# A fused attention and quantised feed-forward kernel: new instruction orders on all engines, the inverse roots apart, fillers on TensorE, the last sets woven

## The chip, the cores and the metric

One core of a Trainium2 chip. The metric is the device time of one execution in microseconds. The kernel before takes 356.12 us (median of 3 runs, 355.98 to 356.35).

## What is computed

Rows are 8192 tokens (32 x 256) of 256 values. The attention mask leaves each query only the keys whose index is congruent to its own modulo the number of queries. Here both counts are 256, so exactly one key is left, the softmax is 1, and attention is a product of the context with Wv and Wout. Wq and Wk have no effect.

```
x = x + tanh(g_xattn) * ((ctx @ Wv) @ Wout + bout)
h = layernorm(layernorm(x)) * ln1_g + ln1_b
h = bitlinear(h, w1, b1)             # 256 -> 1024
h = gelu(h)
h = layernorm(h) * ln2_g + ln2_b
x = x + tanh(g_ffn) * bitlinear(h, w2, b2)   # 1024 -> 256
bitlinear: rows rounded to 8-bit steps of max|row|/127, weights to -1, 0, 1 times mean|w|
```

## The kernel before

The tokens form S = 16 sets; a set is 128 partitions x T = 4 tiles of rows. Wv and Wout are multiplied once into `wvo` (256 x 256), both weight matrices are rounded and transposed on the chip. After that the kernel is a software pipeline of bodies i = -3 to 17. Body i works on several sets at once: the attention of set i+3 (TensorE, L1028), the residual and first statistics of set i+2 (VectorE, L734, L745), the first norm of set i+1, the hidden product and Gelu of set i (L1099, L572), the second norm and its quantising of set i-1 (rows L776, maxima L780), and the second product and the output of sets i-2 and i-3 (L1112, L823).

There is no scheduler. Each engine runs an instruction list written by hand, and semaphores tie the lists together; a wait blocks everything behind it on its engine. So the order in each `body(i)` is what decides who is late. The parts that the change touches:

- GpSimd (L372 to L483). `gain` (L395) multiplies one 128x1024 tile by ln2_g, four times a body; `gain_first` (L386) is one pass as large; `norm_first` (L403, L404) prepares the first variance. `variance` (L413, L414) waits for the fourth squared sum and then makes mean and variance of the second norm. `root` (L378) takes the power -0.5 of both variances, 128x8, in one instruction. `deviations` (L421) and five `split` steps (L437, L442) write means, deviations and scales as three bf16 parts each into `parts`.
- TensorE. `turn_rows` (L1059) transposes `parts` into PSUM, ScalarE copies them (`take_rows`, L563), and then `correction` (L1070, two matmuls into `slot_c`) makes the rank-few terms of a row: the mean and shift of the second norm. `slot_c` holds one row's terms, so a correction waits until VectorE has taken the one before. `hidden` (L1096, L1099) is the first product of a tile, `second_product` and `second_bias` (L1112, L1118) the second, `turn_context` (L948) and `attention` (L1028, L1032) the attention of a half set.
- VectorE. `row` adds the correction to the tile, `row_max` takes its maximum, `final` (L823) writes an output tile. `scales` (L794 to L811) makes quantising scales from maxima and roots in six small operations; its last one, L811, releases ScalarE's `quantise_first` (L544) and GpSimd's `split` of the next body.
- ScalarE. Four pairs of `gelu` (L572) and `square` (L580) a body, the quantising copies (L544, L553), and the copies out of PSUM.
- SyncE (SP) issues the loads, stores and the transposing transfers that turn a quantised tile for the second product (`turn_second`, L243) and the first (`turn_first`, L235), in one queue order. A transfer whose wait isn't met holds up all that stand behind it.

Attention ends at set 15, so TensorE has none from body 13 on. At the end the last set goes through `row`, `scales`, `quantise`, transpose, product and output with little beside it. Its statistics come from one root over four tiles.

## Time and profile before

| what | value |
|---|---|
| median of 3 runs | 356.12 us |
| profiled execution | 356.32 us, its span 354.5 us (1.8 us lie around the span) |
| mean granted TensorE clock | 0.957 of full |
| TensorE busy | 296.9 us, 84% |
| VectorE busy | 294.9 us, 83% |
| ScalarE busy | 277.2 us, 78% |
| GpSimd busy | 265.2 us, 75% |
| DMA | 51.57 MB, mean 145 GB/s |

All engines are busy for three quarters of the span or more, and none is full. In such a kernel the busy share tells little. What is read instead is one body of the pipeline: how long it is, and which chain through the engines closes upon itself in just that time. "Idle before" in a timeline row is the time for which the engine stood still ahead of it, with the instruction that ended the wait. The granted clock of TensorE is 1.00 at 2.4 GHz and 0.50 at 1.2 GHz.

### The profile page before, as it was taken

The page shows a single profiled execution, that of the slowest core. Times are in us where ns is not written, and L with a number is a line of the kernel's source. Part 1 is how long each engine was busy: PE and PEld are TensorE (multiplying, and loading weights), DVE is VectorE, ACT ScalarE, POOL GpSimd, SP SyncE. Part 2 cuts the span into 40 slices and gives each one's busy share as a digit, 9 for nine tenths or more (in the row PEclk, how much of TensorE's full clock was granted, in tenths as well). Part 3 has the DMA queues.
Part 4 walks back from the last instruction along what each step waited for, and adds up shares of the span by engine and source line. Part 5 has one row for each costly group of instructions (what it writes and reads, how often), then busy time and mean ns, then how long its engine had stood idle before and what let it go on. Part 6 is the DMA issues. An engine that isn't in the chain of part 4 may idle for free. (4 is left out here: it accounts for less than half of the span.)

```text
span 354.5 us, 5862 instructions
## 1 busy us (share of the span) xinstructions
PE 296.9 (84%) x1680; PEld 191.7 (54%) x1704; DVE 294.9 (83%) x521; ACT 277.2 (78%) x444; POOL 265.2 (75%) x298
## 2 busy tenths in 40 slices
PE   5998887889898979898989899989998849394566
PEld 4867463537475646465656565655655424242344
DVE  0268898989999999999999999989999948666582
ACT  2155696898989899998989898989898977779340
POOL 4045789997989888989898989898898986738410
PEclk9999999989999999999999999999999978978598
DMA  7956513364858685768666767595555445361457
GB/s 220 324 188 252 151 61 89 118 150 119 189 131 182 111 204 138 170 157 145 182 154 159 160 164 152 165 150 150 112 97 106 104 95 114 74 133 38 82 115 213
DMA packets 98634, 51.57 MB, mean 145 GB/s; under 512 B 87097, under 2 KB 89588, under 8 KB 98602
## 3 DMA queue, kind: packets, MB, share of 16 engines
q1 hardware_dynamic: 97706, 51.15, 59.5%
q8 instruction: 14, 0.23, 0.3%
q10 hardware_dynamic: 896, 0.04, 0.2%
q14 instruction: 18, 0.15, 0.1%
HBM read 21.79 MB, written 8.41 MB: 85 GB/s over the span
## 5 line engine op out<-in xcount | busy, mean ns | idle before, releaser
L395 POOL TENSOR_TENSOR y<-u,g_bc 128x1024 f32<-128x1024 f32 x64 | 151.0, 2368 | 15.3 <-ACT u L572 14.3
L776 DVE TENSOR_TENSOR y<-y,slot_c 128x1024 f32<-128x1024 f32 x64 | 77.7, 1214 | 23.3 <-PE slot_c L1070 23.3
L780 DVE TENSOR_REDUCE amax<-y 128x1 f32<-128x1024 f32 x64 | 78.0, 1218 | 1.8
L553 ACT ACTIVATE q<-y,scale 128x1024 f16<-128x1024 f32 x64 | 70.0, 1144 | 8.2 <-DVE scale L811 8.2
L580 ACT ACTIVATE junk<-u,usum 128x1024 bf16<-128x1024 f32 x64 | 73.7, 1151 | 2.0
L1112 PE MATMUL bank_f<-w2T,q2T 128*128 128x256 f16 x448 | 60.7, 281 | 7.4 <-DVE res L823 5.5
L1112 PEld LDWEIGHTS bank_f<-w2T,q2T 128*128 128x128 f16 x448 | 44.6, 101 | 23.5 <-DVE res L823 6.1
L1028 PE MATMUL slot_a<-wvo,ctxT 128*128 128x256 f32 x208 | 53.4, 386 | 1.0 <-ACT ctxT L515 1.0
L1070 PE MATMUL slot_c<-ln_rows,rows 128*128 128x512 bf16 x119 | 38.1, 397 | 16.6 <-ACT rows L563 7.2
L572 ACT ACTIVATE u<-slot_a,d 128x1024 f32<-128x1024 f32 x32 | 35.5, 1109 | 10.8 <-PE slot_a L1099 9.3
L1028 PEld LDWEIGHTS slot_a<-wvo,ctxT 128*128 128x128 f32 x208 | 36.3, 190 | 11.1 <-ACT ctxT L515 3.6
L1099 PE MATMUL slot_a<-w1T,q1T 128*128 128x512 f16 x128 | 40.5, 400 | 0.5 <-issue 0.2
L544 ACT ACTIVATE q<-h,scale 128x256 f16<-128x256 f32 x64 | 27.4, 500 | 13.8 <-DVE scale L811 13.8
L1099 PE MATMUL slot_b<-w1T,q1T 128*128 128x512 f16 x128 | 38.1, 380 | 0.0
L386 POOL TENSOR_TENSOR h<-x,g_bc 128x1024 f32<-128x1024 f32 x15 | 35.5, 2368 | 0.0
L572 ACT ACTIVATE u<-slot_b,d 128x1024 f32<-128x1024 f32 x32 | 35.1, 1097 | 0.0
L378 POOL TENSOR_TENSOR rstd<-var,half_neg 128x8 f32<-128x8 f32 x18 | 30.2, 1675 | 2.4
L1070 PEld LDWEIGHTS slot_c<-ln_rows,rows 128*128 128x128 bf16 x128 | 10.3, 99 | 33.9 <-issue 17.3
L823 DVE SCALAR_TENSOR_TENSOR res<-bank_f,d,x 128x256 f32<-128x256 f32 x56 | 24.4, 478 | 3.4 <-PE bank_f L1118 3.4
L745 DVE BATCH_NORM_STATS2 bn<-x 128x6 f32<-128x256 f32 x64 | 24.1, 418 | 1.0
L1096 PE MATMUL slot_b<-b_rows,rows 128*128 128x512 bf16 x64 | 24.5, 383 | 0.0
L515 ACT COPY ctxT<-bank_q 128x512 f32<-128x512 f32 x32 | 18.3, 572 | 6.2 <-PE bank_q L948 6.2
(136 smaller groups left out, 430.9 us busy)
## 6 DMA issues: line engine op xcount, KB each, us to landing
c_in<-in_ctx SPq DMA_DIRECT2D x16, 512.0 KB, 4.2
x_in<-in_x SPq DMA_DIRECT2D x16, 512.0 KB, 4.1
out<-res SPq DMA_DIRECT2D x31, 256.0 KB, 2.5
y<-in_L_ffn_w SPq DMA_DIRECT2D x2, 1024.0 KB, 9.0
u<-in_L_xattn_Wkv SPq DMA_DIRECT2D x2, 512.0 KB, 6.2
u<-in_L_xattn_Wout SPq DMA_DIRECT2D x2, 512.0 KB, 7.4
q2T<-q SPq DMA_TRANSPOSE x64, 3.3
g_bc<-in_L_ffn_ln_g SPq DMA_DIRECT2D x1, 512.0 KB, 5.5
```

The source lines that it names most:

```text
L378: nc.gpsimd.tensor_tensor(rstd[:, j % 2, :, :], var[:, :, :], half_neg[:, :, :], ALU.pow) \
L386: nc.gpsimd.tensor_tensor(h1[:, :, :], x1[:, k % SETS, :, :], g1_bc[:, :].unsqueeze(1).to_broadcast([P, T, D]), ALU.mult) \
L395: nc.gpsimd.tensor_tensor(y[:, k % 3, t, :], u[:, t, :], g2_bc[:, :], ALU.mult).then_inc(gain2_done, 1)
L553: nc.scalar.activation(q2[:, t, :], y[:, k % 3, t, :], ACT.Copy, scale=scale[:, (k + 1) % 2, 1, t:t + 1]).then_inc(q2_done, 1)
L572: nc.scalar.activation(u[:, t, :], (slot_a, slot_b)[t % 2][:, :], ACT.Gelu, scale=d12[:, (i - 1) % 3, 0, t:t + 1], accum_out=usum[:, t:t + ...
L580: nc.scalar.activation(junk[:, t % 2, :], u[:, t, :], ACT.Square, scale=-float(H), bias=usum[:, t:t + 1], accum_out=usq[:, t:t + 1]) \
L776: nc.vector.tensor_tensor(line, line, slot_c[:, :], ALU.add).then_inc(y_done, 1)
L780: nc.vector.tensor_reduce(amax[:, 1, t:t + 1], y[:, k % 3, t, :], AX.X, ALU.max, apply_absolute_value=True).then_inc(amax2_done, 1)
L1028: nc.tensor.matmul(acc, ctxT[:, b * P:(b + 1) * P], wvo[:, j, :], start=(j == 0), stop=False)
L1070: terms = nc.tensor.matmul(slot_c[:, 512 * n:512 * (n + 1)], rows[:, (k + 1) % 2, t // 2, :], ln2_rows[:, t % 2, 512 * n:512 * (n + 1)], s ...
L1099: product = nc.tensor.matmul(slot[:, half], q1T[:, t * KD + k, :], w1T[:, k, half], start=False, stop=(k == KD - 1))
L1112: nc.tensor.matmul(product_bank(k, t), q2T[:, t, j, :], w2T[:, j, :], start=(j == 0), stop=False)
```

## The change

- `root` becomes `root_first` (the first norm, 128x4, right after `norm_first`) and `root_second` (128x4, at the end of the body). The mean of `variance` is taken before the wait for the last square.
- `scales` has five operations: the clamp is folded into the two that use its result.
- TensorE's body: `second_product(i-2, 0)` goes from before `hidden(2)` to after `hidden(3)`, `turn_context(i+3, 1)` from after `hidden(3)` to before `hidden(2)`, `second_product(i-2, 1)` before `attention(i+3, 0)`, `turn_context(i+4, 0)` between the two attentions.
- Where a body has no attention (13 to 15), ten 512-column matmuls of no use are issued in its place (`keep_warm`), and eight more ahead of `turn_rows` in bodies 14 and 15.
- SP: `store(i-3, 1)` stands before `turn_second(i-2, 0)`, and the x and context loads and `turn_second(i-2, 1)` and `(i-2, 2)` change places.
- The last set's second norm is done in two halves (`pair_root`), the first two tiles go through `row` before the last two, the woven order ends in a body S+2, and stores stand among the last transposing transfers.
- The start: Wv and Wout are loaded, turned and copied in quarters, the copies shared by VectorE and ScalarE; 22 filler matmuls in place of 14, on a tile that VectorE clears; `sum_weights`, `scale_weights`, residuals and loads reordered, with `deq_inv` gone.

```
 
-            for n in range(2):
-                cols = slice(512 * n, 512 * (n + 1))
+            for n in range(4):
+                cols = slice(256 * n, 256 * (n + 1))
...
                 if live(i):
                     turn_first(i)
+                if live(i - 3):
+                    store(i - 3, 1)
                 if live(i - 2):
                     turn_second(i - 2, 0)
+                    turn_second(i - 2, 1)
                 if live(i + 4):
                     load_x(i + 4)
                 if live(i - 2):
-                    turn_second(i - 2, 1)
-                if live(i - 3):
-                    store(i - 3, 1)
+                    turn_second(i - 2, 2)
                 if live(i + 5):
                     load_context(i + 5)
                 if live(i - 2):
-                    turn_second(i - 2, 2)
...
             turn_second(S - 3, 3)
-            for t in range(T):
-                turn_second(S - 2, t)
-            for t in range(T):
-                turn_second(S - 1, t)
+            turn_second(S - 2, 0)
+            turn_second(S - 2, 1)
+            turn_second(S - 2, 2)
+            turn_second(S - 2, 3)
             store(S - 3, 1)
+            turn_second(S - 1, 0)
+            turn_second(S - 1, 1)
+            turn_second(S - 1, 2)
             store(S - 2, 0)
+            turn_second(S - 1, 3)
...
+                def root_first(k):
+
+                    wait(pool, var1_done, k + 1)
+                    wait(pool, scales_ready, scales_after(k - 3))
+                    nc.gpsimd.tensor_tensor(rstd[:, (k - 1) % 2, 0, :], var[:, 0, :],
+                                            half_neg[:, 0, :], ALU.pow).then_inc(root1_done, 1)
...
-                    nc.gpsimd.tensor_tensor(rstd[:, j % 2, :, :], var[:, :, :], half_neg[:, :, :],
-                                            ALU.pow) \
+                    nc.gpsimd.tensor_tensor(rstd[:, j % 2, 1, :], var[:, 1, :], half_neg[:, 1, :],
+                                            ALU.pow).then_inc(rstd_done, 1)
...
+                def pair_root(h):
+
+                    two = slice(2 * h, 2 * h + 2)
+                    wait(pool, square_done, T * (S - 1) + 2 * h + 2)
...
+                    nc.gpsimd.tensor_tensor(rstd[:, S % 2, 1, two], var[:, 1, two],
+                                            half_neg[:, 1, two], ALU.pow) \
                         .then_inc(rstd_done, 1)
...
+                    wait(pool, gelu_done, T * k + T)
+                    wait(pool, split_steps, split_count(i))
+                    nc.gpsimd.tensor_scalar(stat[:, 2, :], usum[:, :], -1.0 / H, None, ALU.mult)
                     wait(pool, square_done, T * k + T)
                     wait(pool, std_done, i + 2)
...
-                    wait(pool, rstd_done, i + 2)
+                    wait(pool, root1_done, min(i + 2, S))
+                    wait(pool, rstd_done, i)
...
+                elif S <= i <= S + 1:
+                    pair_deviations(i - S)
+                if i >= -1:
                     for n in range(5):
                         split(n)
+                if i == S - 1:
+                    gain(S - 2, 3)
+                    gain(S - 1, 0)
+                    gain(S - 1, 1)
+                    pair_root(0)
+                    return
+                if i == S:
+                    pair_root(1)
+                    return
+                if i == S + 1:
+                    gain(S - 1, 2)
+                    gain(S - 1, 3)
+                    return
+                if i == S + 2:
+                    return
...
@@ -468,16 +528,17 @@
                     gain_first(i + 1)
                 if live(i + 2) and i > 0:
                     norm_first(i + 2)
+                    root_first(i + 2)
...
-                if -1 <= i + 1 <= S:
-                    root(i + 1)
+                    root_second(i + 1)
...
-                    nc.vector.tensor_tensor(amax_g[one], amax[one], power, ALU.mult) \
-                        .then_inc(scale_steps, 1)
...
+                    nc.vector.scalar_tensor_tensor(
+                        out=amax_g[one], in0=amax[one], scalar=1.0 / STEP, in1=power,
+                        op0=ALU.mult, op1=ALU.mult).then_inc(scale_steps, 1)
                     wait(dve, scale_steps, base + 1)
-                    nc.vector.tensor_scalar(amax_g[one], amax_g[one], QEPS, None, ALU.max) \
-                        .then_inc(scale_steps, 1)
-                    wait(dve, scale_steps, base + 2)
                     nc.vector.reciprocal(amax_inv[one], amax_g[one]).then_inc(scale_steps, 1)
                     wait(dve, gelu_done, T * i)
-                    nc.vector.tensor_tensor(d12[:, i % 3, kinds, those], amax_g[one],
-                                            deq[:, kinds].unsqueeze(2).to_broadcast(shape), ALU.mult)
...
                 if i == S:
-                    for t in range(T):
-                        row(S - 1, t)
-                        row_max(S - 1, t)
-                        if t == 2:
-                            scales(slice(1, 2), slice(0, 3))
-                    scales(slice(1, 2), slice(3, 4))
+                    row(S - 1, 0)
+                    row_max(S - 1, 0)
+                    row(S - 1, 1)
+                    row_max(S - 1, 1)
                     final(S - 3, 2)
                     final(S - 3, 3)
-                    for t in range(T):
-                        final(S - 2, t)
-                    for t in range(T):
-                        final(S - 1, t)
+                    row(S - 1, 2)
+                    row_max(S - 1, 2)
+                    scales(slice(1, 2), slice(0, 3), 0)
+                    row(S - 1, 3)
+                    row_max(S - 1, 3)
+                    scales(slice(1, 2), slice(3, 4), 1)
+                    final(S - 2, 0)
+                    final(S - 2, 1)
+                    final(S - 2, 2)
+                    final(S - 2, 3)
+                    final(S - 1, 0)
+                    final(S - 1, 1)
+                    final(S - 1, 2)
+                    final(S - 1, 3)
...
-            zeros = parts[:, :, :].rearrange("p t r -> p (t r)")
-            for n in range(14):
-                nc.tensor.matmul(slot_c[:, 0:T * ROWS], ones_b[:, :], zeros, start=True, stop=True)
+            pe.wait_ge(zeros_ready, 1)
+            for n in range(22):
+                nc.tensor.matmul(slot_c[:, 0:D], junk[:, 0, 0:P], junk[:, 0, P:P + D],
...
-                    wait(pe, rows_copied, k + 4)
-                    nc.tensor.matmul(product_bank(k, t), rows[:, k % 2, t // 2, :],
+                    late = int(k > S - 3)
+                    wait(pe, rows_copied, k + 4 + late)
+                    nc.tensor.matmul(product_bank(k, t), rows[:, (k + late) % 2, t // 2, :],
...
+                def keep_warm(n, first=False):
+
+                    wait(pe, gelu_done, T * (i - 1) + 3 if first else T * min(i, S - 1) + 3)
+                    for _ in range(n):
+                        nc.tensor.matmul(slot_a[:, 512:1024], ident_b[:, :], b1_rows[:, 0, 0:512],
+                                         start=True, stop=True)
...
                 if i == S:
+                    second_product(S - 3, 2)
                     turn_rows()
+                    second_bias(S - 3, 2)
                     correction(S - 1, 0)
                     correction(S - 1, 1)
-                    for t in (2, 3):
-                        second_product(S - 3, t)
-                        second_bias(S - 3, t)
-                    correction(S - 1, 2)
-                    for t in (0, 1):
-                        second_product(S - 2, t)
-                        second_bias(S - 2, t)
-                    correction(S - 1, 3)
-                    for t in (2, 3):
-                        second_product(S - 2, t)
-                        second_bias(S - 2, t)
-                    second_product(S - 1, 0)
+                    second_product(S - 3, 3)
+                    second_bias(S - 3, 3)
...
                 if i == S + 1:
                     turn_rows()
+                    correction(S - 1, 2)
+                    correction(S - 1, 3)
...
+                    return
+                if i == S + 2:
+                    turn_rows()
+                    second_product(S - 1, 0)
...
+                if i > S - 3:
+                    keep_warm(8, True)
...
-                if live(i - 2):
-                    second_product(i - 2, 0)
-                    second_bias(i - 2, 0)
+                if live(i + 3):
+                    turn_context(i + 3, 1)
                 if live(i):
                     hidden(2)
                 if live(i - 1):
                     correction(i - 1, 3)
                 if live(i):
                     hidden(3)
-                if live(i + 3):
-                    turn_context(i + 3, 1)
+                if live(i - 2):
+                    second_product(i - 2, 0)
+                    second_bias(i - 2, 0)
                 if live(i + 1):
                     shift_first(i + 1)
-                if live(i + 3):
-                    attention(i + 3, 0)
                 if live(i - 2):
                     second_product(i - 2, 1)
                     second_bias(i - 2, 1)
                 if live(i + 3):
-                    attention(i + 3, 1)
+                    attention(i + 3, 0)
                 if live(i + 4):
                     turn_context(i + 4, 0)
+                if live(i + 3):
+                    attention(i + 3, 1)
+                else:
+                    keep_warm(10)
```

## Rows read from the trace of the kernel before

**Rows 1.** Busy time by stretch: one middle body, then body 14 (busy TensorE, its loads, VectorE, ScalarE, GpSimd; clock).

```profile
178.43:196.45 18.02, 16.76 (x101) 10.91 (x101) 17.32 (x32) 16.68 (x27) 15.76 (x17) 1.00 0.70 161
287.36:307.66 20.30, 14.73 (x71) 7.54 (x72) 14.21 (x20) 15.77 (x26) 15.38 (x15) 0.83 0.42 92
```

**Rows 2.** Timeline of VectorE in one middle body: start, duration, line, tiles, idle before.

```profile
181.94 1.22 DVE L776 TENSOR_TENSOR y<-y,slot_c 128x1024 f32<-128x1024 f32 x1 [0.21 <-PE slot_c L1070]
...
187.37 1.21 DVE L776 TENSOR_TENSOR y<-y,slot_c 128x1024 f32<-128x1024 f32 x1
...
194.78 0.88 DVE L823 SCALAR_TENSOR_TENSOR res<-bank_f,d,x 128x256 f32<-128x256 f32 x2 [0.18 <-PE bank_f L1118]
...
195.76 0.17 DVE L797 TENSOR_SCALAR amax_g<-amax_g 128x8 f32<-128x8 f32 x1
...
196.29 0.16 DVE L811 SCALAR_TENSOR_TENSOR scale<-amax_inv,rstd 128x8 f32<-128x8 f32 x1
```

**Rows 3.** Timeline of GpSimd, the start of the same body.

```profile
176.17 0.22 POOL L413 TENSOR_SCALAR stat<-usum 128x4 f32<-128x4 f32 x1 [1.21 <-ACT junk L580]
...
176.79 1.67 POOL L378 TENSOR_TENSOR rstd<-var,half_neg 128x8 f32<-128x8 f32 x1
...
178.80 0.29 POOL L437 CAST parts<-stat 128x72 bf16<-128x72 f32 x1
```

**Rows 4.** Timeline of ScalarE, the same body.

```profile
189.26 1.12 ACT L572 ACTIVATE u<-slot_a,d 128x1024 f32<-128x1024 f32 x1
```

**Rows 5.** Timeline of TensorE, the same body.

```profile
180.55 0.28 PE L1059 MATMUL slot_c<-ident_b,parts 128*128 128x128 bf16 x2 [0.30 <-POOL parts L437]
...
186.35 0.59 PE L1070 MATMUL slot_c<-ln_rows,rows 128*128 128x512 bf16 x2 [0.44 <-DVE y L776]
...
189.06 0.59 PE L1070 MATMUL slot_c<-ln_rows,rows 128*128 128x512 bf16 x2
...
191.65 1.03 PE L1028 MATMUL slot_a<-wvo,ctxT 128*128 128x256 f32 x4
...
193.60 1.04 PE L1112 MATMUL bank_f<-w2T,q2T 128*128 128x256 f16 x8
...
194.64 1.13 PE L1028 MATMUL slot_a<-wvo,ctxT 128*128 128x256 f32 x4
```

**Rows 6.** The costliest groups of the page.

```profile
L395 POOL TENSOR_TENSOR y<-u,g_bc 128x1024 f32<-128x1024 f32 x64 | 151.0, 2368 | 15.3 <-ACT u L572 14.3
...
L780 DVE TENSOR_REDUCE amax<-y 128x1 f32<-128x1024 f32 x64 | 78.0, 1218 | 1.8
...
L553 ACT ACTIVATE q<-y,scale 128x1024 f16<-128x1024 f32 x64 | 70.0, 1144 | 8.2 <-DVE scale L811 8.2
```

**Rows 7.** Transposing transfers of L243, issue to landing.

```profile
DMA to landing us min/median/max: 3.0/3.3/6.1
```

**Rows 8.** Timelines of body 14: TensorE, then VectorE, then ScalarE.

```profile
290.79 1.91 PE L1112 MATMUL bank_f<-w2T,q2T 128*128 128x256 f16 x8
...
291.03 1.22 DVE L776 TENSOR_TENSOR y<-y,slot_c 128x1024 f32<-128x1024 f32 x1 [4.32 <-PE slot_c L1070]
...
295.34 1.12 ACT L572 ACTIVATE u<-slot_a,d 128x1024 f32<-128x1024 f32 x1 [2.31 <-PE slot_a L1099]
```

**Rows 9.** Timelines of the end: ScalarE, then VectorE twice.

```profile
325.13 0.19 ACT L580 ACTIVATION_READ_ACCUMULATOR junk<-u,usum 128x1 f32 x1
...
331.70 1.22 DVE L776 TENSOR_TENSOR y<-y,slot_c 128x1024 f32<-128x1024 f32 x1 [6.78 <-PE slot_c L1070]
...
351.64 0.48 DVE L823 SCALAR_TENSOR_TENSOR res<-slot_b,d,x 128x256 f32<-128x256 f32 x1 [0.27 <-PE slot_b L1118]
```

**Rows 10.** Timelines of the start: VectorE twice, then GpSimd.

```profile
17.57 2.29 DVE L681 TENSOR_REDUCE wsum<-y 128x1 f32<-128x2048 f32 x1 [5.31 <-DMA y<-in_L_ffn_w]
...
20.93 0.75 DVE L734 SCALAR_TENSOR_TENSOR x<-slot_b,tg,x_in 128x512 f32<-128x512 f32 x1 [1.08 <-PE slot_b L1048]
...
50.92 1.83 POOL L378 TENSOR_TENSOR rstd<-var,half_neg 128x8 f32<-128x8 f32 x1
```

265 lines of the change are left out of this document (156 added, 109 removed).

## The prediction

> **What bounds it now.** No engine is full over the span, so I read one body of the pipeline and looked for the loop that closes in its time. A middle body lasts 18.02 us [rows 1]; GpSimd's split starts at 53.1 in body 1 (root at 50.92 plus its 1.83 and 0.35 more [rows 10]) and at 287.36 in body 14 [rows 1], so bodies 1 to 13 take 18.02 each.
>
> Then the four engines' timelines of that body. VectorE is busy 17.32 of 18.02 [rows 1] and waits only twice, 0.21 before its first row and 0.18 before the outputs [rows 2]: alone it would need 17.63. GpSimd waits 1.21 for the last square [rows 3]: alone 16.81. So VectorE is nearly full, but a loop sets the pace: TensorE waits for VectorE's second row before the third correction (186.35), issues second product and hidden(2), and ScalarE's third Gelu starts late for it at 189.26 [rows 4, 5]. Two Gelu and square pairs later GpSimd does the mean (176.17), the root (1.67 us from 176.79) and the split from 178.80 [rows 3]; TensorE turns the rows at 180.55 [rows 5], VectorE starts its row at 181.94, 1.39 later [rows 2, 5]. That is one turn of 18.02.
>
> In body 14 the attention is gone, TensorE's clock is granted at 0.83 on average [rows 1], a second product takes 1.91 for 1.04, the first row waits 4.32 and the first Gelu 2.31 [rows 5, 8]; the body takes 20.30.
>
> **The change, middle bodies.** Below, s is the end of a body's scales: 196.29 + 0.16 = 196.45, and 178.43 one body earlier [rows 1, 2].
>
> VectorE: one of six operations goes, 0.17 and a gap of about 0.03 [rows 2]. The four that gain an operand are taken as equal (L811 has that form at 0.16 [rows 2]). 17.63 - 0.20 = 17.43.
>
> The old loop: hidden(2) no longer stands behind a product (1.0: 193.60 to 194.64 [rows 5]) but behind four transposes of a context (estimate 0.44, a quarter of the 1.95 that an attention takes from 191.65 to 193.60 [rows 5]), so ScalarE doesn't wait there, some 0.14. The mean leaves the chain: 0.28 (a stat and its gap [rows 3]). The root on 4 columns in place of 8: its cost lies between 0.93 (proportional, after the 0.2 that a tiny operation such as L413 takes [rows 3]) and 1.67 (all fixed). I take 0.93, since 1.67 is so far above 0.22 that its work must be in the columns. Then this loop is 18.02 - 0.14 - 0.28 - 0.74 = 16.86; with 1.67 it is 17.6.
>
> GpSimd alone: one root of 1.67 becomes two of 0.93 and a gap of 0.1: 16.81 + 0.29 = 17.1.
>
> TensorE's new order is the next loop. The product goes to after hidden(3), ahead of shift, product, two attentions and the next body's first product. From the fourth correction (189.06) to the product at 193.60 it issues 4.54 now [rows 5]; 4.54 includes the 0.44 that leaves this stretch and comes back between the attentions. Add two products (2.0), the second attention (1.95), the next body's product (1.0): turn_rows follows 9.5 after the correction. From there 1.39 to the first row, from 181.94 to the end of the third row at 188.58 it is 6.64 [rows 2], and the hand-over from a row's end to the next correction is taken at 0.15 (an estimate; the third, from 188.58 to 189.06, took 0.48 with TensorE busy). Sum 17.67. That is above VectorE's 17.43, so a wait of about 0.45 stays before the first row, now for TensorE. Middle body: 17.67, less 0.35; 13 bodies: **-4.6**.
>
> SP: store(i-3, 1) now waits for the output that follows the first maximum, at about s + 6.7 (first row at s + 3.6, row, output, maximum, output), and turn_second(i-2, 0) goes out behind it at s + 7.2, not s + 3.9. A landing takes 3.3, at worst 6.1 [rows 7]: it is there at s + 10.5, and TensorE asks at s + 12.1. Hidden, with 1.6 to spare. The second one is 1.25 later, asked for at s + 13.5. The swapped loads are asked for a body later: nothing.
>
> **Bodies 14 and 15.** VectorE has 14.21 of work [rows 1], 0.2 less now. Its first row came 4.3 after s; with the fillers (8 matmuls, 1.7 us, and one product ahead of turn_rows at s + 2.2, split done at s + 2.0) and the clock full it comes at s + 3.6. 3.6 + 14.0 + 0.2 of gaps = 17.8 for 20.3: **-2.5**. In body 15 what counts is ScalarE: the first Gelu came 8.6 after s (295.34 less 286.72, one VectorE wait of 4.32 before 291.03 [rows 8]); now rows are copied at s + 2.5, three quantisations of 1.14 [rows 6] follow, Gelu at s + 5.95. **-2.7**.
>
> **The end.** Counted from the last square, e = 325.32; the last output ends at 352.12, e + 26.8 [rows 9]. Before, the first row waits for mean, root and split of all four tiles: e + 6.4. After, the first two tiles' root and split (GpSimd, two gains of 2.37 earlier [rows 6]) are done before e; ScalarE copies rows after one quantisation, e + 1.4; first row e + 2.1; two rows and maxima at 2.4 each (1.21 and 1.22 overlapping [rows 2, 6]); two outputs 0.8; third row e + 7.6 (its gain ends e + 5.5); scales e + 10.8; fourth row, maximum, scales e + 14.0. The set before's four products end at about e + 15.5, if the first two run at half clock (1.91 each [rows 8]); then two outputs, the store, and only behind it turn_second(15, 3): issued e + 16.7, landed e + 20.0 [rows 7], product 1.0, output 0.48 [rows 9]: e + 21.5. **-5.3**.
>
> **The start.** First residual at 20.93, after 1.08 of waiting for TensorE; w1's sum ends at 19.86 [rows 10]. Quarters and earlier fillers bring TensorE's chain forward by about 1.6 (first transposes one quarter earlier, combines close up), but w1 caps it at 1.1. Two roots of 0.93 instead of one cost 0.2 in each of two bodies; body 0's chain to its root loses mean and half the root as in the middle, 0.28 + 0.74. The reordered sums and loads are taken at nothing: they lie beside the first norms' chain. From both sides 0 and -3: **-1.7**.
>
> Sum: -4.6 - 2.5 - 2.7 - 5.3 - 1.7 = -16.8. The profiled execution took 356.3; 339.5, and by the median, 0.2 lower, **339.3**.
>
> **Rivals.**
> *A, as summed:* 339.3. If TensorE's loop is shorter than I make it and VectorE alone binds (17.43), 336. Chance 0.74.
> *B, the root is fixed cost:* two of 1.67 make GpSimd's body 16.81 + 1.75 = 18.56, 0.89 above A, 13 bodies +11.6, and +1.5 at the start: 352. For it: 1.67 for 8 columns is odd for an engine that does 1024 in 2.37 [rows 6]. Decides from 1.2 us for one root on. 0.10. The Trainium skill (GPSIMD Engine Reference, Instruction dispatch) says that every GpSimd instruction pays a broadcast and a software call before its loop, which speaks against splitting one; no page prices the power itself, and L413's 0.22 bounds that part.
> *C, the fillers don't hold the clock* in 14, 15 and the end: products and hiddens at 1.91 for 1.04 return 2 a body and 1.7 at the end, 345. 0.10. Against: the middle bodies run at 1.00 with gaps of 0.4.
> *D, slower:* SP's queue. If the transfers behind store(i-3, 1) land in 6.1 [rows 7] each time, the product asked for at s + 12.1 starts 1.2 late, delays shift, attentions and turn_rows, and the body is 17.67 + 1.2 = 18.9, or more as the second transfer (s + 8.5 + 6.1) is late by 1.2 again in part: 19.2. 13 x 1.2 over before is +15.6 against the -12.2 of the other parts: 359. Decides from a landing of 4.8; the median is 3.3. 0.04.
> What is left, 0.02, is about no change.
>
> **Numbers.** A measurement tells 0.2% (0.7 us) from nothing. Faster are A, B, C: 0.94. Same 0.02, slower 0.04. The range takes A with its bounds (VectorE bound -3, start and end another -1.5; some of B's root cost +3) and C: 334.5 to 346.
>
> **What would show it.** Each L378-like root at 0.93, GpSimd's body without a wait under 0.2; VectorE's one wait, before the first row, for TensorE; scales 0.66 long; a body of 17.67; clock 1.00 in 14 and 15, each 17.8; the first row of the last set 2.1 after the last square; first residual at 19.9. Wrong if roots take over 1.2, if TensorE waits for a transposing transfer before second_product(i-2, 0), or if bodies 14 and 15 show cold products.

## The result, and the profile after

The changed kernel takes 341.77 us (median of 4 runs, 340.44 to 342.72); the kernel before took 356.24 beside it. The ratio is 0.959, with a 95% interval of 0.955 to 0.963: **4.1% faster**. The forecast was 339.3 with a range of 334.5 to 346, so sign and range held and the size was 2.5 us too good. The profiled execution, the longest of the four, took 342.72 us, with a span of 340.7 against 354.5.

The busy time by stretch comes first: an undisturbed middle body, a longer one, body 14, body 15 up to the end of its scales, and the end (columns as in [rows 1], then the clock, the DMA share and GB/s).

```profile
175.29:192.90 17.61, 16.59 (x101) 10.85 (x100) 17.12 (x30) 16.53 (x27) 16.10 (x17) 1.00 0.80 161
138.63:157.00 18.37, 16.76 (x101) 10.77 (x101) 17.21 (x31) 16.64 (x27) 16.09 (x17) 1.00 0.65 158
281.83:299.45 17.62, 15.84 (x90) 8.50 (x91) 13.87 (x20) 15.58 (x25) 14.76 (x14) 1.00 0.48 105
299.45:315.12 15.67, 14.21 (x82) 7.67 (x82) 11.57 (x17) 14.75 (x25) 10.90 (x18) 1.00 0.54 118
315.12:340.70 25.58, 16.36 (x107) 10.71 (x105) 15.06 (x28) 10.49 (x12) 8.60 (x16) 0.86 0.65 154
```

The middle body is 17.61 for 18.02, body 14 is 17.62 for 20.30 at a clock of 1.00 for 0.83 [rows 1]. The second row is the surprise: the same work in 18.37, at a clock of 1.00.

VectorE in the undisturbed body from 192.90 on, its start, its end and its one wait:

```profile
192.82 0.75 DVE L806 SCALAR_TENSOR_TENSOR x<-slot_a,tg,x_in 128x512 f32<-128x512 f32 x1
...
196.46 1.22 DVE L848 TENSOR_TENSOR y<-y,slot_c 128x1024 f32<-128x1024 f32 x1 [0.21 <-PE slot_c L1155]
...
209.83 0.16 DVE L867 SCALAR_TENSOR_TENSOR amax_g<-amax,rstd 128x8 f32<-128x8 f32 x1
210.03 0.20 DVE L871 RECIPROCAL amax_inv<-amax_g 128x8 f32<-128x8 f32 x1
...
210.35 0.16 DVE L883 SCALAR_TENSOR_TENSOR scale<-amax_inv,rstd 128x8 f32<-128x8 f32 x1
```

The scales are five operations (L867 to L883), and of the two waits of [rows 2] the one before the outputs is gone. So VectorE by itself would need 17.61 - 0.21 = 17.40. GpSimd, the same body:

```profile
191.10 1.04 POOL L394 TENSOR_TENSOR rstd<-var,half_neg 128x4 f32<-128x4 f32 x1
...
193.15 0.29 POOL L478 CAST parts<-stat 128x72 bf16<-128x72 f32 x1 [0.67 <-DVE scale L883]
...
200.09 1.04 POOL L387 TENSOR_TENSOR rstd<-var,half_neg 128x4 f32<-128x4 f32 x1
```

A root on 4 columns takes 1.04 where one on 8 took 1.67 [rows 3]. The mean and the root are done 0.67 before the scales that the split needs: the wait of 1.21 for the last square [rows 3] has become a wait for VectorE. GpSimd alone is at 17.61 - 0.67 = 16.94.

Five of the 12 middle bodies from body 2 on are longer: 18.65, 18.37, 18.29, 18.14 and 17.96 us. In the first of them, body 2, TensorE's turn_rows comes 1.47 late after time that the profile puts to issue, with no wait that it shows, and the granted clock over the next 5 us is 0.66. The gap alone is not what makes the body long: in the run with the store moved (below) it is 1.45, the clock stays at 1.00 and the body takes 17.61. The two stretches behind the gap, the changed kernel's first:

```profile
69.93:74.93 5.00, 4.31 (x13) 1.71 (x15) 3.13 (x8) 4.31 (x5) 4.85 (x4) 0.66 0.76 107
68.49:73.49 5.00, 4.06 (x18) 1.51 (x18) 4.08 (x8) 4.66 (x7) 4.85 (x4) 1.00 0.76 107
```

In the other four TensorE waits for a transposing transfer. One of these, TensorE and then SyncE's queue; the last line is SyncE in an undisturbed body:

```profile
161.19 1.03 PE L1201 MATMUL bank_f<-w2T,q2T 128*128 128x256 f16 x8 [0.66 <-DMA q2T<-q]
```

```profile
156.44 0.34 SPq L254 DMA_DIRECT2D out<-res  x1
156.88 2.29 SPq L248 DMA_TRANSPOSE q2T<-q  x1
159.27 2.52 SPq L240 DMA_TRANSPOSE q1T<-q  x2
...
192.78 1.29 SPq L248 DMA_TRANSPOSE q2T<-q  x1
```

turn_second(i-3,3) stands behind store(i-2,0) of the body before, which waits for an output; and where its issue takes 2.29 instead of 1.29 us, product(i-3,3) has to wait. The issues of 2.26, 2.29, 2.12 and 1.88 us fall in just these four bodies. The kernel before had two waits for a transposing transfer in its middle bodies, 0.82 and 0.75 us, but for another one: turn_second(i-3,2), whose issue took the usual 1.23 or 1.24 us and for which TensorE waited until 6.3 and 6.2 us after it went out.

The experiments are read by four stretches, all from VectorE's timeline: the start of the third last-scales operation (**A**), 13 bodies from there (**B**, bodies 2 to 14), body 15 (**C**), and from there to the start of the last output (**D**). Before: 69.03 + 237.78 + 17.96 + 26.87 = 351.64. After: 66.91 + 232.38 + 15.67 + 22.88 = 337.84. In the twelve experiments A lies between 65.16 and 66.31, whatever they edit, so the changed kernel's profiled execution had a slow start. B moves between executions with the number of longer bodies and with body 2, which takes 17.3 to 17.9 where its clock stays at 1.00 (six of the twelve) and 18.2 to 18.8 where it falls, and D lies between 22.0 and 23.35 where the end is not edited.

### The profile page after: what moved, and what is told of

It reads as the page before. It is cut to its first block, busy times and chain, and to the rows that moved or that the text cites. A ratio compares the mean times of both kernels' runs of the same rounds, so it can differ in the third digit from the quotient of the medians.

```text
span 340.7 us, 6023 instructions
## 1 busy us (share of the span) xinstructions
PE 302.0 (89%) x1735; PEld 193.7 (57%) x1760; DVE 291.7 (86%) x501; ACT 276.1 (81%) x446; POOL 269.2 (79%) x322
## 4 chain that ended last, share of the span: by engine, by line
PE 33%; DVE 28%; issue 12%; DMA 7%; POOL 2%; ACT 1%; SPq 1%; DVEq 0%; POOLq 0%
DVE y L848 14%; PE bank_f L1201 7%; PE slot_a L1111 7%; DVE amax L852 7%; DMA q2T<-q 7%; PE slot_c L1155 4%; DVE res L897 4%; DVE h L833 3%; PE slot_b L1185 2%; PE slot_a L1185 2%; PE bank_q L1027 2%; PE slot_a L1216 2%; ACT rows L629 1%; PE slot_b L1182 1%; PE slot_a L1182 1%
## 5 line engine op out<-in xcount | busy, mean ns | idle before, releaser
L848 DVE TENSOR_TENSOR y<-y,slot_c 128x1024 f32<-128x1024 f32 x64 | 77.7, 1214 | 14.0 <-PE slot_c L1155 13.8
L1201 PE MATMUL bank_f<-w2T,q2T 128*128 128x256 f16 x456 | 59.0, 273 | 3.2 <-DMA q2T<-q 2.4
L1201 PEld LDWEIGHTS bank_f<-w2T,q2T 128*128 128x128 f16 x456 | 43.9, 98 | 20.9 <-issue 6.6
L1155 PE MATMUL slot_c<-ln_rows,rows 128*128 128x512 bf16 x119 | 37.0, 386 | 20.7 <-DVE y L848 10.0
L1111 PE MATMUL slot_a<-wvo,ctxT 128*128 128x256 f32 x208 | 52.2, 381 | 1.0 <-ACT ctxT L581 1.0
L1111 PEld LDWEIGHTS slot_a<-wvo,ctxT 128*128 128x128 f32 x208 | 35.5, 190 | 7.6 <-ACT ctxT L581 1.5
L1185 PE MATMUL slot_a<-w1T,q1T 128*128 128x512 f16 x128 | 39.0, 387 | 0.3
L1155 PEld LDWEIGHTS slot_c<-ln_rows,rows 128*128 128x128 bf16 x128 | 9.0, 97 | 40.6 <-issue 26.8
L897 DVE SCALAR_TENSOR_TENSOR res<-bank_f,d,x 128x256 f32<-128x256 f32 x57 | 25.9, 477 | 2.9 <-PE bank_f L1208 2.9
L581 ACT COPY ctxT<-bank_q 128x512 f32<-128x512 f32 x32 | 18.2, 570 | 7.1 <-PE bank_q L1027 7.0
L1182 PE MATMUL slot_a<-b_rows,rows 128*128 128x512 bf16 x58 | 22.5, 388 | 0.8 <-DMA q1T<-q 0.8
```

The lines of the kernel that those rows point to most:

```text
L848: nc.vector.tensor_tensor(line, line, slot_c[:, :], ALU.add).then_inc(y_done, 1)
L897: nc.vector.scalar_tensor_tensor(out=res[:, k % 2, t, :], in0=product_bank(k, t), scalar=d12[:, (k + 1) % 3, 1, t:t + 1], in1=x1[:, k % SE ...
L1111: nc.tensor.matmul(acc, ctxT[:, b * P:(b + 1) * P], wvo[:, j, :], start=(j == 0), stop=False)
L1155: terms = nc.tensor.matmul(slot_c[:, 512 * n:512 * (n + 1)], rows[:, (k + 1 + late) % 2, t // 2, :], ln2_rows[:, t % 2, 512 * n:512 * (n + ...
L1182: nc.tensor.matmul(slot[:, half], rows[:, i % 2, t // 2, :], b1_rows[:, t % 2, half], start=True, stop=False)
L1185: product = nc.tensor.matmul(slot[:, half], q1T[:, t * KD + k, :], w1T[:, k, half], start=False, stop=(k == KD - 1))
```

## The experiments

**One root again.**

```diff
-                    nc.gpsimd.tensor_tensor(rstd[:, j % 2, 1, :], var[:, 1, :], half_neg[:, 1, :],
+                    wait(pool, var1_done, min(j + 2, S))
+                    nc.gpsimd.tensor_tensor(rstd[:, j % 2, :, :], var[:, :, :], half_neg[:, :, :],
...
-                    root_first(i + 2)
...
```

> Edit: in the steady bodies one root on all 8 columns at the body's end takes the place of the two roots on 4 columns; all else as in the changed kernel. GpSimd's own work per body falls from about 17.1 us by 2 x 1.04 - 1.67 = 0.41, but the root of the first norm now sits behind the deviations, where the scales, the quantised rows and the order loop through TensorE see it. Theory (TensorE's order of steps and VectorE set the body, 17.61 us where nothing disturbs it, and GpSimd has 0.5 to 0.9 of slack ahead of the squares): -0.5 to +1 us for the whole kernel, bodies of 17.6 to 17.65. Rival (the gain came from taking the first root off the chain at the body's end): the body grows by about 1.67 - 1.04 = 0.63, 13 bodies give +8 us, 350.

341.39 us (340.35 to 342.01), undisturbed bodies of 17.61 and 17.62, B = 231.33. The theory holds: in this kernel it no longer matters where the roots stand. The 0.63 that the joined root puts on the chain fits into the 0.67 that GpSimd waited for the scales.

**Small VectorE operations, one and six.**

```diff
+                    nc.vector.tensor_scalar(spare[one], amax_g[one], QEPS, None, ALU.max)
```

> Edit: a sixth small VectorE operation (128x8, into a spare tile that nothing reads) in every scales step, some 0.07 to 0.2 us. Theory (TensorE's loop binds the body by 0.2 and VectorE has a wait of 0.21 ahead of its first row): it is taken out of that wait, bodies stay at 17.61 to 17.65, whole kernel 0 to +1 us. Rival (VectorE's instruction stream is the bound): +0.2 in each of 17 bodies, bodies of 17.8 and +3.4 us.

340.79 us, undisturbed bodies still 17.60 to 17.62, as the theory has it. The operation lengthens the scales by 0.08 only, since it overlaps its neighbours.

> Edit: six small VectorE operations (128x8, into spare tiles that nothing reads) in every scales step; one of them added 0.08 us to the engine's stream and nothing to the body. Six add 0.5. Theory (VectorE alone takes 17.40, so 0.2 of slack ahead of the body's 17.61): body 17.9, +0.3 in each of 13 bodies and what the first and the last scales lose (0.5 each), +4 to +6 us. Rival 1 (the scales' time stands in the loop that sets 17.61): +0.5 in each, body 18.1, +8. Rival 2 (over 0.5 of slack): bodies stay 17.61 and the whole is within +1.5.

343.86 us (342.78 to 344.37), undisturbed bodies of 17.90: 17.40 + 0.5, as the theory has it. In the body from 227.7 to 245.7 VectorE's timeline shows no wait at all. So VectorE's own stream is the second bound, 0.2 below the first. B grew by 1.3 and not by 13 x 0.29 = 3.8. Of the missing 2.5, 1.5 is body 2, which kept its clock here (17.43, where 18.65 + 0.29 was to be expected); for the rest see the next run.

**More TensorE work between the attentions and turn_rows.**

```diff
+                    if t == 2 and k < S - 3:
+                        for _ in range(2):
+                            nc.tensor.matmul(product_bank(k, t), q2T[:, t, 0, :], w2T[:, 0, :],
+                                             start=True, stop=True)
```

> Edit: in the steady bodies the first matmul of product(i-3,2), right ahead of turn_rows, is issued three times instead of once, which leaves its result the same and puts 2 x 0.11 = 0.22 us more on TensorE between the split and turn_rows. Theory (the order loop through TensorE sets 17.61): every undisturbed body becomes 17.8 to 17.85, +2.5 to +3 us. Rival (another loop sets it, and TensorE only waits there): bodies stay 17.61 to 17.65, 0 to +0.5 us.

342.99 us (341.63 to 344.23), undisturbed bodies of 17.82 to 17.84. TensorE with the added matmuls and the step behind them:

```profile
246.18 0.38 PE L1202 MATMUL bank_f<-w2T,q2T 128*128 128x256 f16 x2
246.39 1.04 PE L1205 MATMUL bank_f<-w2T,q2T 128*128 128x256 f16 x8
...
247.38 0.28 PE L1143 MATMUL slot_c<-ident_b,parts 128*128 128x128 bf16 x2
```

0.21 was added (246.18 to 246.39) and each body grew by 0.22: the loop through TensorE's order sets 17.61. Yet B is 232.49 for 232.38, since the longer bodies are fewer and shorter: what B holds above 13 undisturbed ones is 232.38 - 13 x 17.61 = 3.4 us in the changed kernel (1.0 in its first, 2.3 in the four that wait for a transfer) and 232.49 - 13 x 17.83 = 0.7 here. Of the 2.7 between them 1.2 is body 2 with its clock kept (17.62 for 18.65), and the other 1.5 lies in the waits for transfers. So a longer loop takes part of its price from those waits.

**One more root on GpSimd.**

```diff
+                    nc.gpsimd.tensor_tensor(idle_root[:, :], var[:, 0, :], half_neg[:, 0, :],
+                                            ALU.pow)
```

> Edit: GpSimd takes one more root on 4 columns in each steady body, into a tile that nothing reads (+1.04 us of its own work, as its row shows). Theory (GpSimd's own work is 17.1, and 0.5 of slack is left up to 17.61): body 18.1 to 18.2, +0.55 in each of 13 bodies and what the first bodies lose, +7 to +9 us, 349 to 351. This is the price that rival B of the prediction had. Rival (GpSimd has over 1 us of slack): 0 to +1.

343.78 us, B = 234.51: +2.0, neither theory's number. GpSimd in one body, from the second root to the next:

```profile
228.25 1.08 POOL L395 TENSOR_TENSOR rstd<-var,half_neg 128x4 f32<-128x4 f32 x1
...
236.67 1.04 POOL L388 TENSOR_TENSOR rstd<-var,half_neg 128x4 f32<-128x4 f32 x1
237.68 1.01 POOL L533 TENSOR_TENSOR idle_root<-var,half_neg 128x4 f32<-128x4 f32 x1
...
246.20 1.04 POOL L395 TENSOR_TENSOR rstd<-var,half_neg 128x4 f32<-128x4 f32 x1
```

There is no wait from 228.25 to 246.20: GpSimd binds at 17.95, so without the added 1.01 it needs 16.94, as read above, and not the 17.1 of the prediction (the other undisturbed bodies of this run are 17.9 to 18.0). The mean body in B is 18.04 here and 17.88 in the changed kernel, so 0.16 is lost in each, 2.1 in all, where 17.95 - 17.61 = 0.34 would be 4.4; body 2 lost its clock in both. The longer loop again takes part of its price from waits that were there already. Rival B had priced the same step as if the bodies were otherwise undisturbed.

**TensorE's order, alone and with SyncE's.**

```diff
-                if live(i + 3):
-                    turn_context(i + 3, 1)
+                if live(i - 2):
+                    second_product(i - 2, 0)
+                    second_bias(i - 2, 0)
```

The second attention and the turn of set i+4 also go back to their old places.

> Edit: only TensorE's order within a body goes back to that of before: product(i-2,0) ahead of turn_context(i+3,1), attention and the turn of set i+4 at their old places. Theory (the order loop from the split through turn_rows, correction and product to the next split sets 17.61 in the new order): the old loop was summed at 16.86, so the order costs nothing by itself; what it changes is which product waits for q2T. Then bodies of 17.4 (VectorE alone) to 17.7 and -2 to +1 us. Rival (the new order is what gave the gain): bodies return to 17.9 to 18.02 and the kernel loses 3.5 to 5 us, 345 to 347.

376.59 us (three executions from 376.54 to 377.35; a fourth took 384.90), far outside both: bodies 3 to 14 take 19.9 to 21.8. Five of them, of 21.3 to 21.8, had a clock of 0.92, the others 1.00, so some 7 us of the loss go with the lower clock. TensorE's waits of the whole span (us in total, times, longest), then the step itself:

```profile
PE bank_f L1201 <- DMA q2T<-q: 28.1, 16, 2.1
```

```profile
219.87 1.03 PE L1201 MATMUL bank_f<-w2T,q2T 128*128 128x256 f16 x8 [2.07 <-DMA q2T<-q]
```

```profile
215.96 0.35 SPq L254 DMA_DIRECT2D out<-res  x1
216.40 2.65 SPq L248 DMA_TRANSPOSE q2T<-q  x2
```

The transfer goes out at 216.40, right behind store(i-3,1), and product(i-2,0) needs it. This is rival D's mechanism, come true where the product asks for it at the old place. If that is the whole cause, undoing SyncE's order too removes it:

```diff
-                if live(i - 3):
-                    store(i - 3, 1)
                 if live(i - 2):
                     turn_second(i - 2, 0)
-                    turn_second(i - 2, 1)
                 if live(i + 4):
                     load_x(i + 4)
                 if live(i - 2):
-                    turn_second(i - 2, 2)
+                    turn_second(i - 2, 1)
+                if live(i - 3):
+                    store(i - 3, 1)
                 if live(i + 5):
                     load_context(i + 5)
                 if live(i - 2):
+                    turn_second(i - 2, 2)
                     store(i - 2, 0)
```

> Edit: TensorE's order within a body and SyncE's order of issues both go back to those of before (with TensorE's order alone undone the time was 377 us: product(i-2,0) waited 2.07 us for its q2T, in the steady body at 219.87, because SyncE issues store(i-3,1) ahead of turn_second(i-2,0)). Theory (the two orders hang together: the store's wait for the last finals holds back the first transposing transfer, and the later place of product(i-2,0) on TensorE is what hides it): with both back, that wait is gone and the body is 17.4 to 17.8, 338 to 345 us. Rival (the old order of TensorE's steps is itself too long beside the new joined norm): bodies stay above 19 and the time above 365.

341.99 us (341.21 to 342.64), bodies of 17.70: the theory holds. The two orders belong together; together they are worth 0.09 in a body, too little to see in the whole time, and TensorE's old order with SyncE's new one costs 35 us (the reverse was not run). Since undoing both still leaves 17.70, the larger part of 18.02 - 17.61 is not in the order. VectorE's only wait in such a body is the one of [rows 2] before the outputs, which is back:

```profile
198.51 1.22 DVE L848 TENSOR_TENSOR y<-y,slot_c 128x1024 f32<-128x1024 f32 x1
...
208.31 0.87 DVE L897 SCALAR_TENSOR_TENSOR res<-bank_f,d,x 128x256 f32<-128x256 f32 x2 [0.18 <-PE bank_f L1208]
...
209.61 0.16 DVE L883 SCALAR_TENSOR_TENSOR scale<-amax_inv,rstd 128x8 f32<-128x8 f32 x1
```

So the old order has a loop of its own, which can be read from the rows of both kernels: from the third correction (186.35 before, 199.87 here) through TensorE's products and attention to the outputs 8.43 and 8.44, from the outputs to the end of the scales 1.67 and 1.46, from there to the end of the second row 7.77 and 7.66, and 0.15 and 0.14 to the next third correction; 18.02 and 17.70. Of the 0.32 between them 0.21 lies in the stretch of the shortened scales, and 0.11 between the scales and the second row, where the wait of 0.21 before the first row is gone since the split no longer comes late. What stands behind these is the shortened scales, the mean off the chain, the roots apart and one thing more that this run leaves in: VectorE's final(i-3,3) now stands behind row_max(i-1,0). The roots apart are worth nothing beside the others, by the first experiment. The scales, the mean and the place of that output were not undone alone.

**No fillers.**

```diff
-                if i > S - 3:
-                    keep_warm(8, True)
...
-                else:
-                    keep_warm(10)
```

> Edit: the filler products are left out (their results are read by nothing). Theory: the granted clock falls in the bodies 14 and 15 as it did before, body 14 takes 20.3 instead of 17.6 (+2.7) and body 15 up to its last square +2.6, while the end gains some 0.5 because the product behind the fillers starts earlier; +4 to +6 us, 346 to 348. Rival (the bodies 14 and 15 are shorter because of the woven order, not because of the clock): body 14 stays within 0.5 of 17.6 whatever the clock, and the kernel moves by -1 to +1.

343.55 us (342.99 to 344.82), +1.8. Bodies 14 and 15 and the end, by stretch:

```profile
279.73:298.78 19.05, 14.78 (x74) 7.71 (x73) 14.05 (x20) 15.69 (x25) 14.72 (x14) 0.83 0.44 97
298.78:316.60 17.82, 14.20 (x71) 7.33 (x71) 11.74 (x17) 14.57 (x25) 10.75 (x17) 0.81 0.47 103
316.60:341.80 25.20, 16.29 (x100) 10.33 (x99) 15.20 (x28) 10.66 (x13) 8.71 (x16) 0.78 0.75 157
```

The clock falls to 0.83 and 0.81, as in [rows 1], and the two bodies take 19.05 and 17.82 for 17.62 and 15.67: the fillers are worth 1.43 + 2.15 = 3.6 in them, and cost 0.4 at the end (D = 22.51 for 22.88). The whole time rose by less: in the profiled execution A was 0.9 shorter and the twelve bodies ahead of body 14 were 1.2 shorter, as body 2 kept its clock. At the same clock of 0.83 body 14 took 20.30 before, so 1.25 of its gain of 2.68 belongs to the rest of the change and not to the clock; both theories had a part.

**The store behind the transposing transfer.**

```diff
                 if live(i - 3):
                     turn_second(i - 3, 3)
+                    store(i - 3, 0)
...
-                if live(i - 2):
-                    store(i - 2, 0)
...
             turn_second(S - 3, 3)
+            store(S - 3, 0)
```

> Edit: in SyncE's order the store of the first half of set i-3 goes behind turn_second(i-3,3) instead of ahead of it, so the transposing transfer no longer waits for the finals. The quantised row is there at 192.27 and the transfer is issued at 192.78 now, so it can go 0.4 to 0.5 us earlier. Theory (the five longer bodies of 18.0 to 18.7 come from TensorE's wait of 0.5 to 0.74 for this transfer's landing): they shrink to 17.6 to 18.1 and the whole kernel to 339.5 to 340.5 (-1.3 to -2.3); the undisturbed bodies stay 17.61. Rival (whatever lengthens them, the issue's 2.26 us instead of 1.29 among it, is no matter of when it is issued): the sum of the 13 middle bodies stays at 232 to 233 us and the time at 341.3 to 342.

338.19 us (337.83 to 338.49), ratio 0.9456 with an interval of 0.9409 to 0.9503 against the kernel before. SyncE's queue in the undisturbed body whose scales start at 189.92:

```profile
189.48 1.24 SPq L248 DMA_TRANSPOSE q2T<-q  x1
190.77 0.56 SPq L254 DMA_DIRECT2D out<-res  x1
```

The transfer goes out 0.44 before the start of the last scales operation, where it went 0.04 behind it (192.78 to 192.74) in the changed kernel. B is 229.92, 2.5 shorter, and only one wait for q2T is left in it, 0.34 long (three for q1T, whose transfer now goes out later, take 0.20 to 0.41). The mechanism holds: of the 2.5, 1.4 is in the waits for this transfer, at the low end of the 1.3 to 2.3 expected; the other 1.0 is body 2, whose clock stayed at 1.00 here. That is not the store's doing, as the last run below has the same store order and lost it. The whole time fell by 3.6 against the changed kernel and by 3.0 against the halves below, whose kernel before took the same 358.18 us beside it; no execution of those two kernels comes down to any of this one. What the gain holds above 1.4 is not accounted for. In two bodies the issue still takes 2.03, and 1.5 to 1.8 in four more, so what lengthens it is not the store's wait.

**Wv and Wout in halves again.**

```diff
-            for n in range(4):
-                cols = slice(256 * n, 256 * (n + 1))
+            for n in range(2):
+                cols = slice(512 * n, 512 * (n + 1))
...
-                pe.wait_ge(wv_in[n], 16)
+                pe.wait_ge(wv_in[n // 2], 16)
...
```

> Edit: Wv and Wout come in two halves each again; all else as in the changed kernel. In the changed kernel w1 lands at 18.60, 1.0 later than before, and the first residual stands at 20.81 against 20.93 before, so the quarters gained 0.1 there and not the 1.0 that was predicted. Theory (the first residual is bound by w1's landing and its issue behind four more DMAs, so the quarters bring next to nothing): the first residual within 0.4 of 20.8 and the whole kernel within 0.7. Rival (the quarters carry the start's gain of 1.9): the first residual 0.5 to 1.2 later, +0.7 to +2 us.

341.17 us (340.07 to 342.13), A = 65.78, first residual at 19.35; with quarters it came between 18.82 and 20.81. Quarters show no gain outside this spread.

**The end.**

```diff
+                    keep_warm(8)
                     correction(S - 1, 3)
...
-                    keep_warm(10)
+                    keep_warm(10 if i < S - 1 else 4)
...
+            turn_second(S - 1, 3)
             store(S - 2, 0)
-            turn_second(S - 1, 3)
```

> Edit, at the end alone: 8 filler matmuls ahead of correction(15,3), 4 in place of 10 at the end of body 15, and turn_second(15,3) ahead of store(14,0) on SyncE's queue. Theory (the end, e+23.4 against the e+21.5 that the prediction summed, is late by the 10 fillers ahead of the product and turn_rows, by set 14's products at half speed, 1.92 us each at 325.63 and 327.55, and by turn_second(15,3) behind the store): products of 1.04 instead of 1.92, turn_second(15,3) issued some 1.5 to 2 earlier, end at e+20.5 to e+21.5, -2 to -3 us. Rival (the scales at e+14.97 set the end and the transfers cannot go sooner): 0 to -0.7.

339.18 us (338.71 to 340.37). D = 21.82 for 22.88, barely under the 22.0 to 23.35 of the kernels with the old end, so this part is 0.2 to 1.5, less than the 2 to 3 expected; the 2.7 that A and B are shorter here lie in stretches that the edit does not touch. With four fillers in place of ten ahead of it, the first row of the last set comes 1.94 after the scales of body 15 for 2.95. TensorE, from the last split's wait on:

```profile
328.20 0.28 PE L1143 MATMUL slot_c<-ident_b,parts 128*128 128x128 bf16 x2 [2.53 <-POOL parts L478]
328.32 1.04 PE L1201 MATMUL slot_a<-w2T,q2T 128*128 128x256 f16 x8
329.36 1.91 PE L1201 MATMUL bank_f<-w2T,q2T 128*128 128x256 f16 x8
331.28 1.71 PE L1201 MATMUL slot_b<-w2T,q2T 128*128 128x256 f16 x8
```

Set 14's products ran at 1.03 and 1.04, but behind the 2.53 us of waiting for the split the clock was lost again, now for set 15's: one product of 1.04, then 1.91 and 1.71. So the last run fills that gap too (8 fillers into slot_b ahead of the last turn_rows) and takes the store's new place with it.

> Edit: the store behind the transposing transfer (338.2 by itself) and the end's three edits (339.2 by itself) together, and 8 more fillers ahead of the last turn_rows, where TensorE waited 2.53 us for the split and then ran two of set 15's products at 1.91 and 1.71 us. Theory (the two gains lie in different stages and add: -3.6 and -2.6 against the changed kernel's 341.8, and the last products at 1.04 give another 0.5 to 1.0 unless the last transfer's landing binds them): 334.8 to 336. Rival (they share the end, where a shorter body only moves the same wait): 337.5 to 338.2.

337.11 us (335.72 to 339.08, 6 runs), ratio 0.9471 with an interval of 0.9438 to 0.9505. The end is right: clock 1.00 over it, products of 1.03 and 1.04 throughout, D = 20.82, 1.2 below the lowest of the kernels with the old end.

```profile
324.90 1.89 PE L1216 MATMUL slot_b<-b_rows,ident_b 128*128 128x512 bf16 x8
327.58 0.28 PE L1143 MATMUL slot_c<-ident_b,parts 128*128 128x128 bf16 x2 [0.79 <-POOL parts L478]
327.86 1.03 PE L1201 MATMUL slot_a<-w2T,q2T 128*128 128x256 f16 x8
328.84 1.04 PE L1201 MATMUL bank_f<-w2T,q2T 128*128 128x256 f16 x8
```

The sum is neither full nor absent: 4.7 us faster than the changed kernel where the parts add to 6.2, as B came out 0.7 longer than with the store's new place alone, with bodies of 18.64 (body 2, its clock lost again) and 18.00. Its interval overlaps that of the store's run, and its ratio, 0.9471, is not below that run's 0.9456, so the end's edits are shown by D and not by the whole time. It is the lowest median of the study, and it beats both kernels.

## Why the prediction was right, and where it was off

The profiled executions differ by 13.8 up to the last output: 2.1 in A, 2.8 in bodies 2 to 13, 2.6 in body 14, 2.9 in body 15 up to the last square, 3.4 behind it. The prediction had 16.8. The errors do not cancel; the terms for the 13 bodies and for the end were too large by 1.4 and 1.9, and the rest slightly too small.

- **Middle body: right.** 17.67 was summed over TensorE's new order, 17.61 is measured, and the loop is the one named: 0.21 more on TensorE gave 0.22 a body. VectorE alone was put at 17.43 and is at 17.40. GpSimd was put at 17.1 and is at 16.94, though each root took 1.04 for the 0.93 taken: the 16.81 that the prediction started from still held a second wait, 0.17 before a gain at 190.61. The bounds 0.93 and 1.67 held, the value nearer to the lower.
- **The old loop, 16.86: incomplete.** The sum followed the Gelus and GpSimd to the split, and that path did get short: with both orders undone the split waits 0.65 for the scales. But the 0.18 before the outputs [rows 2] was taken for idle time, and it belongs to the loop through the outputs that closes in 17.70. By the prediction's sums the old order would have left VectorE alone at 17.43, below the new order's 17.67; it is 17.70, above 17.61. The forecast of 17.67 does not rest on this, as it was summed over the new order.
- **13 bodies, -4.6: mis-sized.** The step "13 bodies" multiplied the undisturbed body and left out the waits for turn_second(i-3,3). From A on, 12 bodies fell from 217.53 to 214.76, 2.8 for the 0.35 x 12 = 4.2 summed: above the undisturbed body they hold 0.29 each, where those of before, at 18.02, held 0.11. Two thirds of the 0.29 are waits for that transfer, one third is body 2 and its clock. The prediction's "18.02 each" was an average: body 1 took 16.78 from split to split, and four of the others 18.15 to 18.53. The SP step looked at store(i-3,1) and turn_second(i-2,0) alone, found 1.6 to spare, and was right there (no wait for it in the changed kernel); the one that became late was the transfer whose place did not change, while TensorE came to ask earlier.
- **Body 14, -2.5: right** at -2.6, 17.62 for 17.8. The first row waits 3.57 for 4.32. **Body 15, -2.7: right** at -2.9: the first Gelu comes 5.9 after the scales (5.95 summed). The price of rival C, 2 a body, was 1.43 and 2.15.
- **The end, -5.3: mis-sized**, -3.4. Counted again from the last square, e = 314.91:

```profile
313.49 2.32 PE L1216 MATMUL slot_a<-b_rows,ident_b 128*128 128x512 bf16 x10
315.65 1.04 PE L1201 MATMUL bank_f<-w2T,q2T 128*128 128x256 f16 x8
316.52 0.28 PE L1143 MATMUL slot_c<-ident_b,parts 128*128 128x128 bf16 x2
...
325.63 1.92 PE L1201 MATMUL bank_q<-w2T,q2T 128*128 128x256 f16 x8
327.55 1.92 PE L1201 MATMUL slot_a<-w2T,q2T 128*128 128x256 f16 x8
...
336.66 1.03 PE L1201 MATMUL slot_b<-w2T,q2T 128*128 128x256 f16 x8 [0.92 <-DMA q2T<-q]
```

  The step "first row e + 2.1" had the split and the copy of the rows, but not the ten fillers that run up to 315.65 and the product behind them: it came at e + 3.0. From there each step is later, third row e + 8.6 for 7.6, last scales e + 15.0 for 14.0, products of set 14 done e + 17.0 for 15.5, and turn_second(15,3) issued at e + 18.5 for 16.7. The last output's end is e + 23.4 for 21.5. Cold products were forecast as two of 1.91; there were two of 1.92 and one of 1.45.
- **The start, -1.7: near in the profiled execution, wrong in its steps.** A, which holds body 1 and its forecast 0.35 too, fell by 2.1 there and by 2.7 to 3.9 in the others, so the term was rather too small. Quarters show no gain (the run with halves), and "two roots in each of two bodies" is one body: there is a single root on 4 columns in each of bodies -2 and -1 (25.68 and 30.85), and only body 0 has two (48.09 and 49.75). What brings A its gain was not taken apart.
- **Rivals.** A held, with its loop. B's condition (1.2 us for a root) did not hold, and its price for added GpSimd work was too high: 1.01 a body cost 2.0, where 13 undisturbed bodies at GpSimd's 17.95 would make 4.4. D's mechanism is real, but needs TensorE's old order: then 2.07 a body.

## What to carry to other kernels

Where engines are within 4% of each other, a body's time is the undisturbed loop plus the waits that come and go: count the bodies that have one, and look at the clock of each, before multiplying, and price an added or removed cost against the mean body. When one consumer's step moves forward or back in an order, look at every transfer that it comes to ask for, above all those whose issue stands behind a wait for something else; here one store's place on the queue was worth more than the whole reordering of TensorE. Idle time ahead of matmuls is worth filling wherever the next ones are on the path, but fillers queued in front of a step that is about to be released delay it.

## What the runs showed of the hardware

- **A root's cost.** 1.67 us for 8 columns [rows 3] and 1.04 for 4 on 128 partitions, which makes 0.16 a column and 0.41 that does not depend on them; the roots on 2 columns at the end, 0.73 each, lie on the same line. The Trainium skill (GPSIMD Engine Reference, Instruction dispatch) speaks of a fixed part of every GpSimd instruction; these rows agree that there is one, but it is the smaller part of a root on 8 or 4 columns, as halving the 8 saved 38%.
- **A VectorE operation of 0.12 us took 2.10.** VectorE, then GpSimd, in body 0:

```profile
45.24 0.20 DVE L871 RECIPROCAL amax_inv<-amax_g 128x8 f32<-128x8 f32 x1
45.36 2.10 DVE L873 SCALAR_TENSOR_TENSOR d<-amax_g,deq 128x8 f32<-128x8 f32 x1
```

```profile
42.66 4.78 POOL L432 TENSOR_TENSOR y<-u,g_bc 128x1024 f32<-128x1024 f32 x2
47.41 0.24 POOL L440 TENSOR_SCALAR stat<-moments 128x4 f32<-128x4 f32 x1
```

  It ends at 47.46, where GpSimd's pair of gains ends at 47.44. The Trainium skill (SBUF — State Buffer, Who interferes with whom) says that a VectorE instruction with two SBUF inputs and a GpSimd instruction that reads SBUF exclude each other; these rows agree. Beside a root they do not, though it reads SBUF too. VectorE and GpSimd in the kernel before:

```profile
195.57 0.15 DVE L794 TENSOR_TENSOR amax_g<-amax,rstd 128x8 f32<-128x8 f32 x1
```

```profile
194.81 1.67 POOL L378 TENSOR_TENSOR rstd<-var,half_neg 128x8 f32<-128x8 f32 x1
```

  That operation and the three others of those scales with two SBUF inputs took 0.11 to 0.17 while the root was under way, up to 196.48. Why a gain holds VectorE up and a root does not stays open.
- **The issue of one transposing transfer takes 1.23 to 1.33 us in most bodies and 1.5 to 2.3 in some**, in the kernel before, the changed one and the run with the store moved. In the last two it is mostly turn_second(i-3,3), in the kernel before mostly turn_second(i-2,2). What lengthens it stays open.
- **The same gap can cost the clock or not.** Behind a gap of 2.53 us of a waiting TensorE (328.20 in the end's run) the granted clock was 0.50 from 329.36 to 331.28, and behind one of 0.79 (327.58 in the last run) it stayed at 1.00. In body 2 a gap of 1.47 was followed by 0.66 over 5 us in the changed kernel and by 1.00 in the run with more TensorE work, with 18.65 and 17.62 us for the body. What decides it stays open.
